# A Mamba and mixture-of-experts block on one core: bias inside the product, softplus by halves out of the side banks, epsilon on GpSimd, and one table of places for the whole program

## The reference, cut to what matters

```
def ssm_branch(xz_half, z, ...):                 # once forward, once on the reversed sequence
    x = silu(causal_conv4(xz_half) + conv_b)     # [tokens, 512]
    dbc = x @ Wx.T                               # 64 step-size columns, 16 of B, 16 of C
    delta = softplus(dbc[:, :64] @ Wdt.T + b_dt) # [tokens, 512]
    h[t] = exp(delta[t] * A) * h[t-1] + delta[t] * B[t] * x[t]     # 512 channels x 16 states
    y[t] = sum over states of h[t] * C[t]
    return (y + Dp * x) * silu(z)

x = x + layernorm(0.5 * (forward + backward) @ W_out.T)
f = layernorm(x)
x = x + layernorm(shared_expert(f) + sum over the top 2 of 8 experts of share * expert(f))
```

## Time and profile before

| | us |
|---|---|
| median of 3 runs | 4935.37 |
| lowest and highest of them | 4934.9 and 4937.17 |
| the profiled execution | 4934.7 |
| its span | 4933.5 |
| busy in it: DVE | 4110.9 (83%) |
| POOL | 3603.1 (73%) |
| PE | 3478.7 (71%) |
| ACT | 2994.4 (61%) |

### The profile page before, as it was taken

The page is one execution under the profiler, slowest core; times in us unless marked ns, Lnnn a source line. Parts: engine busy times, 40 slices in busy tenths (PEclk is TensorE's granted clock), DMA queues, the critical chain, the costliest instruction groups (busy, mean ns, idle before and its releaser), DMA issues.

```text
span 4933.5 us, 52400 instructions
## 1 busy us (share of the span) xinstructions
PE 3478.7 (71%) x16720; PEld 2528.6 (51%) x16720; DVE 4110.9 (83%) x4080; ACT 2994.4 (61%) x4068; POOL 3603.1 (73%) x2076
## 2 busy tenths in 40 slices
PE   3466766787677867777767866778668876787575
PEld 1344444665446645565446644566446654475354
DVE  2999999898989989898989989898998989898200
ACT  3454555776657755677657765578556766575243
POOL 1698877878877888778878788777878788788111
PEclk8556676998779967898769877798778977798687
DMA  4221232455325642456315553355424563264144
GB/s 135 90 80 61 90 137 69 167 179 186 120 88 183 202 162 82 141 173 208 127 68 188 174 172 122 109 187 193 150 72 164 175 195 129 76 206 155 62 148 148
DMA packets 360958, 687.40 MB, mean 139 GB/s; under 512 B 30817, under 2 KB 204394, under 8 KB 356586
## 3 DMA queue, kind: packets, MB, share of 16 engines
q1 hardware_dynamic: 348394, 650.48, 39.4%
q0 software_dynamic: 12288, 33.57, 2.1%
HBM read 513.04 MB, written 170.92 MB: 139 GB/s over the span
## 4 chain that ended last, share of the span: by engine, by line
DVE 34%; issue 19%; POOL 18%; PE 15%; ACT 9%; DMA 4%; SPq 1%; DVEq 0%; POOLq 0%; ACTq 0%
DVE h L834 16%; POOL drive L1299 10%; DVE y L849 9%; PE h_t L680 4%; PE side L812 2%; POOL y L1307 2%; DVE side L909 2%; POOL work L1360 2%; DVE stats L887 2%; POOL xu L1321 1%; POOL xs_dram L1349 1%; ACT decay L1038 1%; PE side L804 1%; PE side L715 1%; DMA work<-y_dram 1%
## 5 line engine op out<-in xcount | busy, mean ns | idle before, releaser
L1299 POOL TENSOR_TENSOR drive<-xu,b_row 128x1024 f32<-128x1024 f32 x1024 | 2427.8, 2381 | 363.7 <-DVE h L834 360.1
L834 DVE TENSOR_TENSOR_SCAN h<-decay,drive 128x1024 f32<-128x1024 f32 x1024 | 2333.0, 2278 | 123.8 <-POOL drive L1299 68.0
L680 PE MATMUL h_t<-ident,h 128*128 128x128 f32 x8192 | 1546.3, 330 | 887.8 <-DVE y L849 590.4
L680 PEld LDWEIGHTS h_t<-ident,h 128*128 128x128 f32 x8192 | 1155.6, 169 | 1402.5 <-DVE y L849 811.3
L1038 ACT ACTIVATE decay<-delta,neg_a 128x1024 f32<-128x1024 f32 x1024 | 1143.9, 1118 | 867.2 <-DVE h L834 824.1
L849 DVE SCALAR_TENSOR_TENSOR y<-h_t,c_col,y 128x512 f32<-128x512 f32 x1488 | 1068.5, 734 | 220.4 <-PE h_t L680 217.9
L1307 POOL TENSOR_TENSOR y<-y,scaled 128x512 f32<-128x512 f32 x496 | 641.3, 1293 | 323.6 <-ACT scaled L1056 317.1
L812 PE MATMUL side<-expert_w,work 128*128 128x256 f32 x1472 | 405.1, 427 | 56.4 <-issue 35.2
L804 PE MATMUL side<-xn_t,expert_w 128*128 128x128 f32 x2944 | 411.9, 287 | 46.4 <-DMA expert_w<-in_w 21.5
L1056 ACT ACTIVATE scaled<-h_t,c_col 128x512 f32<-128x512 f32 x496 | 341.1, 688 | 147.3 <-PE h_t L680 146.1
L804 PEld LDWEIGHTS side<-xn_t,expert_w 128*128 128x128 f32 x2944 | 376.7, 201 | 61.5 <-DVE xu L909 19.3
(11 more groups left out here) (145 smaller groups left out, 3855.7 us busy)
## 6 DMA issues: line engine op xcount, KB each, us to landing
expert_w<-in_w SPq DMA_DIRECT2D x384, 512.0 KB, 4.1
b_row<-b_dram SPq DMA_DIRECT2D x256, 512.0 KB, 3.9
dx_dram<-prep_work SPq DMA_DIRECT2D x64, 512.0 KB, 2.9
delta_dram<-prep_work SPq DMA_DIRECT2D x64, 512.0 KB, 2.8
delta<-delta_dram SPq DMA_DIRECT2D x64, 512.0 KB, 4.3
work<-xs_dram SPq DMA_DIRECT2D x40, 512.0 KB, 4.3
ys_dram<-work SPq DMA_DIRECT2D x40, 512.0 KB, 6.1
xz_dram<-prep_work SPq DMA_DIRECT2D x32, 512.0 KB, 3.0
```

The source lines that it names most:

```text
L680: t = pe.e.transpose(h_t[i % N_H_T][:, c * P:(c + 1) * P], h[:, gn % 2, c, tb * P:(tb + 1) * P], ident[:, :])
L834: dve.e.tensor_tensor_scan(o, a, v, 0.0, ALU.mult, ALU.add).then_inc(scanned, 1)
L1299: pool.e.tensor_tensor(drive[:, k % N_DRIVE, :], xu[:, w % 2, c, :], b_row[:, gn % N_B_ROW, :], ALU.mult).then_inc(drive_made, 1)
```

## The change

**Bias in the product.** `dbc` and `wdt_sb` get a 97th row: ones in `dbc`, b_dt in `wdt_sb`; the rows of B and C meet weights of 0. `dt_mm` multiplies 97 rows instead of 64, and `dt_bias` is gone. POOL sets the new rows at the start; SP waits for that and then loads b_dt in two transfers of 512 single elements.

**Softplus and the second D term by halves.** `softplus` takes its Abs from the side bank, 512 tokens at a time, and `delta` reads the product in the bank and the log part in SBUF. The bank is now emptied by `delta`. For the backward D term a new piece on ACT, `dx_scale`, writes Dp * x into a side bank by halves, and `dx_add` on DVE adds the stored part.

**Epsilon on GpSimd.** DVE ends with the variance; POOL adds the epsilon and then takes the power.

**Table of places.** `AT` has a place for every piece of every batch; `HEAD` and `TAIL` are gone. A second table, `BANK_USE`, gives the order in which the side banks are used, turn and turn about.

```diff
 AT = {
-    "softplus": [-560, -352, -143, -32, 976, 1121, 1712, 1936],
...
+    "softplus": [-736, -720, -688, -656, -576, -48, -16, -15, 992, 1008, 1504, 1520, 1648, 1680, 1840, 1872, 3473,
...
-EMPTIED_BY = {..., "dt_mm": "dt_bias",
+EMPTIED_BY = {..., "dt_mm": "delta", "dx_scale": "dx_add",
...
+    for use, (product, _) in filled.items():
+        bank_of[product] = use % N_SIDE
+        if use >= N_SIDE:
+            bank_before[product] = filled[use - N_SIDE][1]
...
-                    mm = pe.e.matmul(bank[:, :], wdt_sb[:, w % 2, c * P:(c + 1) * P],
-                                     dbc[0:DTR, s * BANK:(s + 1) * BANK], start=True, stop=True)
+                    mm = pe.e.matmul(bank[:, :], wdt_sb[:, w % 2, c * P:(c + 1) * P],
+                                     dbc[:, s * BANK:(s + 1) * BANK], start=True, stop=True)
...
-                    op = dve.e.scalar_tensor_tensor(out=prep_half, in0=prep_half, scalar=0.0, in1=dx_buf[1],
-                                                    op0=ALU.max, op1=ALU.add)
+                    if c:
+                        dve.wait_ge(done["u_mul"], nth("u_mul", w, c - 1))
+                        dve.wait_ge(done["delta_store"], 16 * nth("delta_store", w, c - 1))
...
+                    op = dve.e.scalar_tensor_tensor(out=prep_half[:, half_of], in0=side[bank_of["dt_mm", index]][:, :],
+                                                    scalar=0.0, in1=dx_buf[1][:, half_of], op0=ALU.max, op1=ALU.add)
...
-                    op.then_inc(var_step[piece], 1)
-                    dve.wait_ge(var_step[piece], nth(piece, kind, at))
-                    op = dve.e.tensor_scalar(rstd[:, 0:n], mv[:, 0:n, 1], EPS, None, ALU.add)
...
-                    op = dve.e.scalar_tensor_tensor(out=dx_buf[c % 2], in0=xu[:, 1, c, :], scalar=chan_col(1, c, CHAN_D),
-                                                    in1=dx_buf[c % 2], op0=ALU.mult, op1=ALU.add)
+                    op = dve.e.tensor_tensor(its, side[bank_of["dx_scale", index]][:, :], its, ALU.add)
...
+                elif piece == "dx_scale":
...
+                    bank = free_bank(act, piece, index)
+                    op = act.e.mul(bank[:, :], xu[:, 1, c, s * BANK:(s + 1) * BANK], chan_col(1, c, CHAN_D))
...
-                elif piece == "dt_bias":
...
-                    act.e.activation(log_part, prep_half, ACT.Abs).then_inc(soft_step, 1)
+                    act.e.activation(log_part, side[bank_of["dt_mm", index]][:, :], ACT.Abs).then_inc(soft_step, 1)
...
+                    pool.e.tensor_tensor(rstd[:, 0:n], mv[:, 0:n, 1], small[:, 0:n], ALU.add
+                                         ).then_inc(rstd_step[piece], 1)
...
+            pool.e.memset(wdt_sb[DTR:NP + 1, :, :], 0.0).then_inc(pool_set, 1)
+            pool.wait_ge(pool_set, 1)
+            pool.e.memset(dbc[NP:NP + 1, :], 1.0).then_inc(pool_set, 1)
+            pool.wait_ge(pool_set, 2)
+            pool.e.memset(small[:, :], EPS).then_inc(pool_set, 1)
...
+            sp.wait_ge(pool_set, 6 + E + 2)
+            for d in range(2):
+                k = d * NCH + CHAN_B_DT
+                sp.e.dma_start(wdt_sb[NP:NP + 1, d, :], chan[:, k:k + 1].rearrange("e a -> a e"),
+                               allow_slow_non_contiguous=True).then_inc(dt_bias_in, 16)
```

462 lines of the change are left out of this document (220 added, 242 removed), and 333 rows, old and new, of tables (AT, BANK_USE, TAIL).

## The result

The changed kernel takes 4785.9 us (median of 4 runs, 4781.6 to 4797.5) against 4936.3 of before in the same series: a ratio of 0.9697, 95% interval 0.9677 to 0.9716. Run once more beside later experiments it took 4784.2 (5 runs). The time went the way that was forecast; its size was missed.

The account below looks back on a forecast made before the run. DVE was taken to set the pace in the eight batches, the last batch's expert layers in the tail. 4934.7 - 110 (arithmetic) - 25 (router) + 15 (burst) + 27 (tail) + 1 (head) = 4843 us; range 4800 to 4900.

Parts of the forecast that it names:

- The arithmetic: DVE in the eight batches: delta 42, dx_add 28.9 and epsilon 39.5 us saved, 110 in all, bounds 100 and 115.
- the PSUM input as the reason: delta and dx_add on DVE: with one input in PSUM they no longer wait for POOL, about 0.68 us a half.
- rival (d): delta and dx_add on DVE: the new form waits for POOL as the old one did, 4914 us; 3%.
- The tail: After the last scan: batch 6's expert chain of 40.4 us starts behind the last scaled, +27 us, bounds +20 and +34.
- The burst on POOL: Batches 2 to 6: twelve scatters in a row make DVE stand 7.3 us; +15 us, bounds 0 and +50.
- The head: Before the first scan: memset wait and single-element loads cost 5.3 us, 4 given back; net +1, bounds -4 and +6.
- The step that failed: Table of places: nearly every side instruction moves, but only router stretch, scatters on POOL and tail have a price.
- Rival (b): Batches: the table does more, a tenth less DVE idle time in each of seven, 40 us, giving 4803; 12%.
- The router's term: Router stretch: PE work stands inside the wait for slots, 25 us gained over seven batches, 0 to 40.
- a microsecond off DVE counts in the eight batches: Eight batches, 4447.4 us: DVE sets the pace, so its savings count there and nowhere else.
- rival (c): Side banks held longer stall PE and h_t: 192 uses at 1 us give 5035, decisive from 0.48 a use; 7%.
- the slow rate of PSUM: delta on DVE: by the skill's rule PSUM reads would lose 16 us, time 58 us above the forecast.

Follow-up runs that it names:

- experiment 3: Changed kernel with delta and dx_add halves reading both tensor inputs from SBUF, none from PSUM (delta leaves out the step-size product): 4918.3 us.
- experiment 4: Arithmetic of the kernel before at the places and in the bank order of the changed kernel: 4911.0 us against 4937.1 before.
- experiment 9: Changed kernel with the four pieces of the forward x_proj product bunched again at units 103 to 104 in five batches: 4798.8 us.
- experiment 8: Changed kernel with the first mix_turn of each batch going again through the bank that the slots chain empties, all places kept: 4832.7 us.
- experiment 1: Kernel before with only the epsilon moved from DVE to GpSimd, table of places as before: 4902.5 us, 34.6 below before.
- experiment 5: Kernel before, old table, with delta and softplus by halves, bias in the product and epsilon on POOL, dx_add as before: 4948.5 us, ratio 1.0032.
- experiment 2: Changed kernel with the epsilon back on DVE, all else kept: 4807.8 us.
- experiment 6: Kernel of experiment 5 with the first load of the sorted tokens three places earlier on SyncE in seven batches: 4920.1 us, 28 below experiment 5.
- the tail's edit: Changed kernel with batch 6's last gelu, second layers, store and gathers started earlier at the end: 4779.2 us against 4784.2.

## Why the prediction was wrong in size

**What held.** The arithmetic: 110 forecast, 112.3 on the lines, with 0.68 us a half (0.69 and 0.68 were taken); the PSUM input as the reason (experiment 3); rival (d) is dead. The tail: +27 forecast, +24.7 measured. Its chain in the profile:

```profile
4392.12 0.69 ACT L1328 ACTIVATE scaled<-h_t,c_col 128x512 f32<-128x512 f32 x1 [2.25 <-PE h_t L946]
4392.82 1.28 ACT L1524 ACT_TABLE_LOAD   x1
...
4437.96 0.69 DVE L1280 TENSOR_TENSOR acc<-side,acc 128x512 f32<-128x512 f32 x1 [4.75 <-PE side L1058]
```

The last comb ends 45.8 us behind the last `scaled`, where 40.4 were taken from the end of the kernel. Counted from the end of the batches it is 31 us later than before, and the tail only 24.7 longer; the rest of the tail is 7 us shorter, for which no run gives a reason. So two errors, of 4 and 7 us, partly cancel, and that +27 came so close is in part luck. The burst on POOL: +15 forecast, and waits for drives grew by 17.4, though a single one is 11.4 and not 7.3. The head: +3.5 against +1, within its bounds. The two loads of single elements take 1.25 us together (row below) and not 3.8 (2.2 for their elements and two issues of 0.8), and the first token load is issued 2.6 us later than before and not 5.3. But the first scan is 3.5 us later, so of the 4 us that I gave back nothing shows. Here too two errors partly cancel.

```profile
6.00 1.25 SPq L1881 DMA_DIRECT2D wdt_sb<-in_chan  x2
```

**The step that failed** is the one on the table: it "moves nearly every side instruction, and three places of it have a price". All others had the price nothing. The waits for `h_t` fell by 78 us, and by 72 with the table alone (experiment 4); outside the router stretch nothing had been counted. What was left out is above all one stretch, units 104 to 119: 8.2 to 8.5 us of waits in each of six batches before (and 5.8 and 2.8 in the first and the last), next to the 12.4 us of the router that were priced, and 4.8 in all eight after. These 54 us are about what the forecast missed, 57. Experiment 9 shows how such a place works and that one product there is worth 15 us: PE's side product stands ahead of a transposition that DVE is already waiting for. Rival (b) was this case, with a tenth of the idle time and 12%; it was right in direction and nearest in time, and should have been the forecast. Its tenth of the idle time was a guess, and no place was named for it.

**The router's term** was about right: 25 us were taken, and the waits for `h_t` in its stretch fell by 32 (38 in the repeat), within the 0 to 40. The 48 us of experiment 8 aren't its size, since the router stands at other places there, ahead of POOL's burst and the token load. They show that at these places the bank matters about twice as much as I would have said; that a late PE delays the scatters and the load behind it is argued from the waits, not tested.

**A premise with a limit:** "a microsecond off DVE counts in the eight batches". In the new table it does (experiment 3: 149 us more of busy DVE in the batches, 134 us more of time), and in the old one it does where nothing else hangs on the instruction (experiment 1: 37 us of busy DVE, 35 us of time). But delta by halves out of the bank gained nothing in the old table (experiment 5), and rival (c), banks held until delta, was real there: PE waited 104 us for delta, 0.8 us a use. In the changed kernel PE waits 19.5 us for delta and 8.3 for dx_add in the whole program, 0.14 us a use, where the point of decision was 0.48. So the two halves of this change can't be priced apart and added:

| | old arithmetic | new arithmetic |
|---|---|---|
| old table | 4935 | 4948 (4920 with the early load; dx_add old) |
| new table | 4911 | 4784 |

By my sum the table was worth +18 (slower). Measured it is worth -26 with the old arithmetic. With the new one it is some -135, an estimate: 4948, less the 29 us that dx_add would give, against 4784.

**One input in PSUM.** The Trainium skill, "VectorE: DVE Perf Modes", § Rules for kernel authors, would take the slow rate of PSUM for a cost. The rows show none for this type: the shortest delta is 659 ns with one input in PSUM and 655 with both in SBUF. The Trainium skill, "SBUF — State Buffer", § Who interferes with whom, says that a DVE instruction with two SBUF inputs contends with a GpSimd instruction that reads SBUF, and that one with at most one SBUF input, outside what it calls the 2-port perf modes, does not. Experiment 3 agrees: maxima of 693 ns against 8622. "One SBUF input" alone doesn't decide it, though: the epsilon, a TENSOR_SCALAR with one input in SBUF, reached 2114 ns before and 3065 in experiment 2. Whether it was in such a mode no run shows.

**What stays open.** Which pieces besides the x_proj product made DVE wait in units 104 to 119. How the 102 us of idle time in experiment 5 divide between the banks and the load beyond the 28 of experiment 6; the placement of the halves in the old table is mine, and a better one may lose less. Whether the tail's edit is worth its 5 us can't be told from these runs.

## What to carry to other kernels

When instructions of the pacing engine are made faster, list every transfer and bank release that came just in time before: a wait of another engine that cost nothing (PE's 34 us for the tokens in the kernel before) becomes the pace, and the saving is gone unless the order is made anew. Before a new order is priced, add up the waits of the pacing engine stretch by stretch over the whole period, and look in each stretch whether the new order removes their cause; here the second largest sum, 8.4 us a batch in sixteen units, got no price, and it was the gain that was missed. And before spreading a burst, check whether the engine that does it has slack in that stretch; if not, the wait only moves.

## What the runs showed of the hardware

- Both inputs in SBUF cost a DVE instruction 1168 and 1712 ns in the median beside a busy POOL, and 8622 at worst; one in PSUM, 680 and never over 693. Undisturbed they are equal (655 and 659 ns for 512 columns of f32).
- Halving such an instruction does not halve its waiting: in one table of places 64 chunks of delta cost 112 us (1746 ns each, experiment 4) and 128 halves 171 us (1335 ns each, experiment 3). In the kernel before the 64 chunks cost 130 us.
- Two loads of 512 single elements occupied SyncE for 0.62 us each, and the load behind them was issued in 0.62 us.
